# Centred output weights, an addition straight from PSUM, small norm operations on VectorE, and a new table of latencies

## The reference

```python
x = x + layernorm(attn(layernorm(x)))
x = x + layernorm(ffn(layernorm(x)))

def attn(x):
    q = silu(x @ Wq1 @ Wq2)                    # 256 -> 128 -> 512
    f = sigmoid(x @ Wk1 @ Wk2); v = x @ Wv
    a = exp(log_sigmoid(f)); k = 1 - a
    h = scan over tokens of  h = a*h + k*v
    out = q * h
    out = out * rsqrt(mean(out*out) + 1e-6) * norm_w
    return out @ Wo                            # 512 -> 256

def ffn(x):                                    # six blocks
    for i in range(6):
        x = gelu(x @ W1[i].T + B1[i]) @ W2[i].T + B2[i] + x
        if i < 5: x = layernorm(x) * LN_G[i] + LN_B[i]
```

## Time and profile before

| | us |
|---|---|
| median of three runs | 656.39 |
| lowest, highest | 656.38, 657.34 |
| the profiled execution's own time | 656.95 |
| its span, first to last instruction | 655.2 |

### The profile page before, as it was taken

The page is one execution under the profiler, slowest core; times in us unless marked ns, Lnnn a source line. Parts: engine busy times, 40 slices in busy tenths (PEclk is TensorE's granted clock), DMA queues, the critical chain, the costliest instruction groups (busy, mean ns, idle before and its releaser), DMA issues.

```text
span 655.2 us, 8823 instructions
## 1 busy us (share of the span) xinstructions
PE 637.2 (97%) x3015; PEld 530.1 (81%) x3015; DVE 448.2 (68%) x747; ACT 409.7 (63%) x678; POOL 284.2 (43%) x253
## 2 busy tenths in 40 slices
PE   7898999999999999999999999999999999999996
PEld 5677788888888888888888888888888888888886
DVE  6778665678567767758765777677687757764635
ACT  4988986788756555557555575555675545564433
POOL 6988442669516611338232175212372321222203
PEclk9999999999999999999999999999999999999999
DMA  8120000001101200003000021000020000000001
GB/s 283 66 97 1 1 1 1 1 1 66 65 0 48 82 1 2 0 1 117 13 2 0 1 64 66 1 1 1 0 66 1 0 2 0 2 1 32 33 1 66
DMA packets 8685, 19.36 MB, mean 30 GB/s; under 512 B 1600, under 2 KB 4672, under 8 KB 8640
## 3 DMA queue, kind: packets, MB, share of 16 engines
q1 hardware_dynamic: 8352, 18.53, 8.4%
q10 hardware_dynamic: 288, 0.26, 0.1%
HBM read 16.69 MB, written 2.10 MB: 29 GB/s over the span
## 4 chain that ended last, share of the span: by engine, by line
PE 89%; POOL 5%; issue 3%; DVE 1%; ACT 1%; DMA 0%; POOLq 0%; ACTq 0%; DVEq 0%
PE BK L457 43%; PE BK L742 39%; PE BK L566 2%; PE BK L752 2%; POOL WL L344 1%; POOL QB L551 1%; POOL SB L575 1%; PE BK L431 1%; PE BK L612 1%; PE BK L579 0%; POOL WL L298 0%; DMA X<-in_x 0%; PE BK L792 0%; PE BK L629 0%; ACT R L384 0%
## 5 line engine op out<-in xcount | busy, mean ns | idle before, releaser
L728 ACT ACTIVATE HH<-BK,B 128x512 fp32r<-128x512 f32 x192 | 132.4, 690 | 203.7 <-PE BK L457 203.3
L734 DVE TENSOR_TENSOR HL<-BK,HH 128x512 fp32r<-128x512 f32 x192 | 131.0, 684 | 82.6 <-ACT BK L731 82.2
L457 PE MATMUL BK<-XH,WL 128*128 128x512 f32 x416 | 163.7, 393 | 0.0
L457 PE MATMUL BK<-XH,WH 128*128 128x512 f32 x416 | 162.3, 390 | 0.0
L457 PE MATMUL BK<-XL,WH 128*128 128x512 f32 x416 | 162.0, 389 | 0.0
L742 PE MATMUL BK<-HH,WL 128*128 128x512 f32 x368 | 146.7, 399 | 0.0
L742 PE MATMUL BK<-HL,WH 128*128 128x512 f32 x368 | 143.7, 390 | 0.0
L742 PE MATMUL BK<-HH,WH 128*128 128x512 f32 x368 | 143.2, 389 | 0.0
L731 ACT ACTIVATE BK<-BK,B 128x512 f32<-128x512 f32 x192 | 125.6, 654 | 0.0
L457 PEld LDWEIGHTS BK<-XH,WH 128*128 128x128 f32 x416 | 78.1, 188 | 17.0
L457 PEld LDWEIGHTS BK<-XL,WH 128*128 128x128 f32 x416 | 78.2, 188 | 16.1
(11 more groups left out here) (121 smaller groups left out, 823.3 us busy)
## 6 DMA issues: line engine op xcount, KB each, us to landing
STG<-in_w SPq DMA_DIRECT2D x24, 512.0 KB, 3.7
out<-R SPq DMA_DIRECT2D x16, 128.0 KB, 1.9
X<-in_x SPq DMA_DIRECT2D x3, 512.0 KB, 7.8
R<-in_wv SPq DMA_DIRECT2D x1, 512.0 KB, 5.8
STG<-in_wo SPq DMA_DIRECT2D x1, 512.0 KB, 6.2
X<-in_x ACTq DMA_DIRECT2D x2, 128.0 KB, 3.0
X<-in_x SPq DMA_DIRECT2D x2, 128.0 KB, 2.8
R<-in_wq SPq DMA_DIRECT2D x1, 256.0 KB, 3.3
```

Of the source, the lines that this page charges most:

```text
L457: r = e.matmul(dst, s, m, start=first and i == 0, stop=last and i == len(todo) - 1)
L728: lambda e, ev=ev, hs=hs, bias=bias: e.activation(HH[:, hs, :], bank_of[ev][:, :], ACT.Gelu, bias=bias),
L734: lambda e, ev=ev, hs=hs: e.tensor_tensor(HL[:, hs, :], bank_of[ev][:, :], HH[:, hs, :].bitcast(f32), ALU.subtract), ("hlo", n, j))
```

## The change

- **Wo is centred.** Row means of Wo over its 256 output features are subtracted before it is scaled by norm_w and split. The projection then has mean zero over features, so l2 needs no subtraction of a mean. The scaling moves from one GpSimd operation to VectorE: a sum (128x1024 to 128x4), a multiplication by -1/256, and four operations of 128x256 that add the mean and multiply by norm_w. They wait until `ulo` of tile 0 is issued, and have keys from -3.
- **l2_nm is gone.** In its place `x1`, four on VectorE, computes X = PA * RS + X straight from the accumulators. The GpSimd addition is gone, and the next tile's first projection (and the feed-forward pass 2) waits for x1.
- **Small operations.** VE goes to VectorE for all three norms; NM is gone; NBS = mean * -1 * RS is one VectorE operation, and is not made for l2. The power stays on GpSimd. `first_norm` and the norms of the last passes (688, 802) are as they were.
- **Keys.** l3's statistics, norm and transposes get lower keys (Z + 6, 9.5, 11 for Z + 7, 11.5, 13).
- **The planner.** `LASTS` has other durations, `HOP` goes from 0.21 to 0.07, and a table `FREE` is new: the planner gives an engine free that much before the end of its instruction. A DMA issue counts 0.45 for 0.1.

```diff
-LASTS = {"sync": 0.1, "scalar": 0.6, "vector": 0.68, "gpsimd": 1.31, "tensor": 1.36,
-         "_st": 0.41, "_mv": 0.15, "_nm": 0.42, "_rs": 1.03, "_ve": 0.2, "_ng": 0.2, "_nb": 0.2, "ms": 0.15,
-         "turn": 0.88, "zk": 0.69, "zq": 0.69, "rms": 0.45, "proj": 1.44, "t2": 0.72, "scan": 1.31, "olo": 0.85,
...
-         "ghi": 0.69, "gf": 0.65, "ctr": 0.84, "xlo": 0.8, "sum1": 1.41, "sum2": 1.41, "mu": 0.15, "va": 0.15,
-         "vae": 0.15, "rsd": 3.0, "ft": 0.25, "fin0": 0.4, "fin1": 0.83}
-HOP = 0.21
+LASTS = {"sync": 0.45, "scalar": 0.62, "vector": 0.68, "gpsimd": 1.3, "tensor": 1.52,
+         "_st": 0.41, "_mv": 0.16, "_nm": 0.6, "_rs": 1.05, "_ve": 0.16, "_nb": 0.16, "ms": 0.16,
+         "turn": 0.6, "turned": 0.6, "zk": 0.84, "zq": 0.84, "rms": 0.6, "proj": 1.6, "ua": 1.07, "u": 0.62,
+         "t1": 0.6, "t2": 0.72, "a": 0.73, "scan": 1.28, "olo": 0.8, "o": 1.32, "ssum": 1.36,
...
+         "wo_scaled": 0.41, "wo_sum": 1.15, "wo_mean": 0.16, "bias": 0.23, "nw": 0.22,
+         "sum1": 1.45, "sum2": 1.45, "mu": 0.27, "va": 0.27, "vae": 0.16, "rsd": 2.92, "nn": 0.74, "y": 0.74,
...
+FREE = {"sync": 0.0, "scalar": 0.11, "vector": 0.09, "gpsimd": 0.05, "tensor": 0.16}
+HOP = 0.07
 LAND = 2.1
 RATE = 3e5
@@
-        clock[e] = t + (0.1 if done in moved else lasts(e, done))
+        spent = 0.45 if done in moved else lasts(e, done)
+        clock[e] = t + spent - FREE[e]
         if done:
             issued.add(done)
-            ends[done] = clock[e]
+            ends[done] = t + spent
             if done in moved:
-                wire = max(wire, clock[e]) + moved[done] / RATE
+                wire = max(wire, t + spent) + moved[done] / RATE
@@
-        op("scalar", -98, [("one",)], lambda e: e.activation(WARM[:, :], ONE[:, :], ACT.Gelu), ("warm",))
+        op("scalar", -96.5, [("one",)], lambda e: e.activation(WARM[:, :], ONE[:, :], ACT.Gelu), ("warm",))
@@
-        op("gpsimd", -2, [("ldw_o",), ("nw",)],
-           lambda e: e.tensor_tensor(STG[:, 0, :].rearrange("p (m n) -> p m n", m=4),
-                                     STG[:, 0, :].rearrange("p (m n) -> p m n", m=4),
-                                     NW[:, :].unsqueeze(2).to_broadcast([128, 4, 256]), ALU.mult),
-           ("wo_scaled",))
-        split(0.5, raw["o"], WH[:, 1, 2560:3584], WL[:, 1, 2560:3584], "wo", [("wo_scaled",)])
+        op("vector", -3, [("ldw_o",), ("after", ("ulo", 0, 1))],
+           lambda e: e.tensor_reduce(WM[:, :], STG[:, 0, :].rearrange("p (m n) -> p m n", m=4),
+                                     mybir.AxisListType.X, ALU.add), ("wo_sum",))
+        op("vector", -2.9, [("wo_sum",)],
+           lambda e: e.tensor_scalar(WM[:, :], WM[:, :], -1 / 256, 1.0, ALU.mult, ALU.mult), ("wo_mean",))
+        for m in range(4):
+            op("vector", -2.8 + 0.1 * m, [("wo_mean",), ("nw",)],
+               lambda e, m=m: e.tensor_scalar(STG[:, 0, 256 * m:256 * m + 256], STG[:, 0, 256 * m:256 * m + 256],
+                                              WM[:, m:m + 1], NW[:, m:m + 1], ALU.add, ALU.mult), ("wo_scaled", m))
+        split(0.5, raw["o"], WH[:, 1, 2560:3584], WL[:, 1, 2560:3584], "wo", [("wo_scaled", m) for m in range(4)])
@@ stats
             if name == "l2":
-                op("gpsimd", key + gap * 4 + 0.5, [*every, ("ms", t)],
+                op("vector", key + gap * 4 + 0.5, [*every, ("ms", t)],
                    lambda e: e.tensor_tensor(VE[:, t, :], MV[:, t, :, 1], MS[:, t, :], ALU.add), (name + "_ve", t))
             else:
-                op("gpsimd", key + gap * 4 + 0.5, every,
+                op("vector", key + gap * 4 + 0.5, every,
...
-            op("gpsimd", key + gap * 4 + 0.55, every,
-               lambda e: e.tensor_scalar(NM[:, t, :], MV[:, t, :, 0], -1.0, 1.0, ALU.mult, ALU.mult), (name + "_ng", t))
...
-            op("gpsimd", key + gap * 4 + 0.7, [(name + "_rs", t), (name + "_ng", t)],
-               lambda e: e.tensor_tensor(NBS[:, t, :], NM[:, t, :], RS[:, t, :], ALU.mult), (name + "_nb", t))
+            if name != "l2":
+                op("vector", key + gap * 4 + 0.7, [(name + "_rs", t), *every],
+                   lambda e: e.scalar_tensor_tensor(NBS[:, t, :], MV[:, t, :, 0], -1.0, RS[:, t, :], ALU.mult, ALU.mult),
+                   (name + "_nb", t))
@@ proj
-                   + ([("after", ("proj", t, m - 1))] if m else [("l2_nm", t - 1, c) for c in range(4)] if t else []), proj, ("proj", t, m))
+                   + ([("after", ("proj", t, m - 1))] if m else [("x1", t - 1, c) for c in range(4)] if t else []), proj, ("proj", t, m))
@@
-            norm(Z + 4.5, "l2", t, R[:, t], p_of, 0.3, [("turned", k) if t == 0 else ("turn", "l1", t, k) for k in range(2)])
             for c in range(4):
-                op("gpsimd", Z + 5.5 + 0.6 * c, [("l2_nm", t, c)],
-                   lambda e, t=t, c=c: e.tensor_tensor(X[:, t, c, :], X[:, t, c, :], R[:, t, c, :], ALU.add),
-                   ("x1", t, c))
-            stats(Z + 7, "l3", t, x_of, lambda c, t=t: [("x1", t, c)], 0.4)
-            norm(Z + 11.5, "l3", t, R[:, t], x_of, 0.3, [("x1", t, c) for c in range(4)])
-            turn(Z + 13, "l3", t, [("l3_nm", t, c) for c in range(4)], ("mm1", t, 7))
+                op("vector", Z + 4.5 + 0.4 * c, [("l2_rs", t), *x_in(c)],
+                   lambda e, t=t, c=c: e.scalar_tensor_tensor(X[:, t, c, :], p_of(c), RS[:, t, c:c + 1], X[:, t, c, :],
+                                                              ALU.mult, ALU.add), ("x1", t, c))
+            stats(Z + 6, "l3", t, x_of, lambda c, t=t: [("x1", t, c)], 0.4)
+            norm(Z + 9.5, "l3", t, R[:, t], x_of, 0.3, [("turned", k) if t == 0 else ("turn", "l1", t, k) for k in range(2)])
+            turn(Z + 11, "l3", t, [("l3_nm", t, c) for c in range(4)], ("mm1", t, 7))
@@ mm2 of pass 2
-                            [("l2_nm", NT - 1, c) for c in range(4)] if n == 2 else
+                            [("x1", NT - 1, c) for c in range(4)] if n == 2 else
```

More of the change, by code:

```diff
@@ L28 @@
 F_STEP = 2.62
[L32 to L38 removed]
+LASTS = {"sync": 0.45, "scalar": 0.62, "vector": 0.68, "gpsimd": 1.3, "tensor": 1.52,
+         "_st": 0.41, "_mv": 0.16, "_nm": 0.6, "_rs": 1.05, "_ve": 0.16, "_nb": 0.16, "ms": 0.16,
+         "turn": 0.6, "turned": 0.6, "zk": 0.84, "zq": 0.84, "rms": 0.6, "proj": 1.6, "ua": 1.07, "u": 0.62,
+         "t1": 0.6, "t2": 0.72, "a": 0.73, "scan": 1.28, "olo": 0.8, "o": 1.32, "ssum": 1.36,
+         "f_rs": 0.75, "f_nm": 0.41, "x1": 0.47, "ghi": 0.7, "gf": 0.66,
+         "wp_hi": 1.06, "wv_hi": 1.06, "wo_hi": 1.06, "wq1_hi": 0.42, "wk1_hi": 0.42,
+         "wp_lo": 1.45, "wq2_lo": 1.45, "wk2_lo": 1.45, "wv_lo": 2.4, "wo_lo": 2.4, "wq1_lo": 0.42, "wk1_lo": 0.8,
+         "wo_scaled": 0.41, "wo_sum": 1.15, "wo_mean": 0.16, "bias": 0.23, "nw": 0.22,
+         "sum1": 1.45, "sum2": 1.45, "mu": 0.27, "va": 0.27, "vae": 0.16, "rsd": 2.92, "nn": 0.74, "y": 0.74,
+         "ft": 0.38, "inj": 1.9, "end": 1.6, "fin0": 0.41, "fin1": 0.75,
+         "mhalf": 0.1, "quarter": 0.1, "half": 0.1, "one": 0.06, "warm": 2.9, "idle_in": 0.53, "spin": 5.7}
+FREE = {"sync": 0.0, "scalar": 0.11, "vector": 0.09, "gpsimd": 0.05, "tensor": 0.16}
+HOP = 0.07
 LAND = 2.1
@@ L221, in sandwich @@
         MS = sb("MS", [128, NT, 4])
-        NM = sb("NM", [128, NT, 4])
+        WM = sb("WM", [128, 4])
         NBS = sb("NBS", [128, NT, 4])
```

1 line of the change is left out of this document (removed).

## The result

The changed kernel took 661.3 us in the median (661.06 to 662.05, four runs), the kernel before 656.47 beside it: a ratio of 1.0072 with a 95% interval of 1.0055 to 1.009. It is 4.8 us slower, where 4.6 us faster was predicted. The profiled execution has a span of 660.0 us against 655.2.

The account below looks back on a forecast made before the run. PE, busy 97% of the span, was taken as the bound, so gains come from its idle time at 10 to 72 us; -1.8 - 1.0 - 1.7 - 1.2 + 0.7 + 0.4 = -4.6 us gave 651.8 us, range 647.5 to 658.0.

Parts of the forecast that it names:

- first projections: PE's waits for OL and XH at the first projections: shorter with small operations off GpSimd, 0 to 3.0 us, taken 1.8.
- last projection of tile 0: PE's wait for OL after tile 0's fourth scan: GpSimd's relief starts the product earlier, gain 0 to 1.2 us, taken 1.0.
- l2 of tile 0: PE's 2.5 us wait for the accumulators' last read: x1 on VectorE ends it sooner, 0 to 2.5 us, taken 1.7.
- l3 of tile 0: PE's 1.5 us wait at tile 0's third norm: chain 4 us shorter, gain 0 to 1.5 us, taken 1.2.
- Wo block's length: Sum, mean and scalings added on VectorE ahead of attention work at about 15 us: cost 0 to 3.0 us, taken 0.7.
- lock: Small two-operand VectorE operations wait for long GpSimd ones on a shared SBUF port: at most 2.1 us, taken 0.4.
- after 72 us: Rest of the span: VectorE still has room, so reordering costs only if PE waits for a bank; no cost counted.
- o can start about 1.2 us earlier at least: First attention product on GpSimd, at 25.61 us before: without small operations ahead of it, starts about 1.2 us earlier.
- costs nothing: Wo's low part made about 4 us later frees a weight slot later; taken as covered, otherwise 4 us.
- GpSimd as the bottleneck: From 10 to 72 us GpSimd, busy 52.90, was as full as PE; its busy time should fall by 8 us or more.
- B: Rival, chance 0.17: the Wo block on VectorE delays the first tile 3.0 us, gaps behind OL and XH stay; 659 us.
- the first scan after 24 us: Sign that the wo term is wrong, with PE idle near 20 us; the first scan started at 21.97 before.

Follow-up runs that it names:

- e9: Changed kernel in its planned order, Wo block left out, so Wo is neither centred nor scaled: 661.69 us, ratio 1.0059.
- e10: Changed kernel in its planned order, wo_lo and eight feed-forward weight subtractions on GpSimd replaced by zero writes that read nothing: 657.53 us, ratio 0.9997.
- e11: Kernel before in its planned order, the same GpSimd subtractions replaced by zero writes that read nothing: 655.84 us, ratio 0.9978.
- e14: Kernel before in its kept order, only VE and NBS put on VectorE and NM gone: 658.11 us, ratio 1.0007.
- e1: Changed kernel, its order planned with the table of durations of the kernel before: 661.87 us, ratio 1.0068.
- e2: Kernel before, no instruction changed, planned with the new durations, FREE and HOP: 664.09 us, ratio 1.011.
- e3: Kernel before with only the Wo block moved to VectorE, planned anew with the old table: 664.04 us, ratio 1.01.
- e4: Kernel before with only VE and NBS on VectorE and NM gone, planned anew with the old table: 667.98 us, ratio 1.0161.
- e8: Kernel before, planned anew with only the planned start of tile 1's attention changed, 20.6 for 20.4: 658.46 us, ratio 1.0023.
- e18: Kernel before in its kept order, x1 from PSUM on VectorE in all four tiles, Wo not centred, l3's statistics behind the scan: 656.19 us, ratio 0.9986.
- e5: Changed kernel's order, with tile 1's statistics, norm, transposes and first products moved ahead of the Wo block and first projection: 660.67 us, ratio 1.0052.

## Why the prediction was wrong

The sum came out with the wrong sign. Each term, with what came; the measured figures are sums over starts, as above, for the stretch named:

| term | forecast | measured |
|---|---|---|
| first projections | -1.8 | +5.7 (20 to 40 us), an estimated 1 to 1.5 of it the clock |
| last projection of tile 0 | -1.0 | -1.4 (40 to 50 us): the wait of 1.21 us is gone |
| l2 of tile 0 | -1.7 | -1.4 (50 to 60 us): its wait is 0.82 for 2.46 |
| l3 of tile 0 | -1.2 | -0.1 (60 to 72 us): its wait is gone, waits for OL (1.13) and XL (1.04) came |
| Wo block's length | +0.7 | 0 to 0.9, in this order (e9) |
| lock | +0.4 | about +3.5 of the loss, part of the first line (e10, e11) |
| after 72 us | 0 | +2.5 |

**The step that failed first** is "o can start about 1.2 us earlier at least". It was worked out in the order of before: take the small operations away, and everything behind them moves up. Even there it fails: e14 keeps that order, and o starts 0.27 us earlier and not 1.2, because the freed queue then waits for a scan that the small operations on VectorE have made late. And the kernel after doesn't run in that order. The first o starts at 26.31, later than 25.61, and it no longer is what the projection waits for, which is OH behind tile 1's norm and OL behind two more scans. The prediction named the new planning and priced it only beyond 72 us; in the first 72 it followed each chain as if nothing else were placed anew. Experiments e1 to e4 and e8 show that planning anew can have the largest price: +1.5 us for a shift of 0.2 us in one start, +7.2 for new durations with not one instruction changed. In the kept order the parts are worth +0.5 (small operations) and -0.9 (x1 in e18), and in the new one the Wo block at most 0.9. The Wo block in the kept order, and both kept-order edits in one kernel, weren't run.

**The second is the size of the lock.** It was priced for small operations that wait, 2.1 us at most, of which 0.4 went into the sum. What weighs is the other kind: long scans and OL held by long GpSimd subtractions. The scans alone are 8 x (1.709 - 1.244) = 3.7 us longer in the first stage, in the earlier trace rows the first of them 1.32 and now 2.07. For the first scan the cause is that wo_lo slid from 15.41 to 20.63, from before the scans to beside them; e9 puts this down to where the new plan sets Wo's high part on ScalarE, not to the time that the Wo block takes. The prediction, which found that the later wo_lo "costs nothing", looked only at who waits for it, not at whom it would run beside.

**The third is GpSimd as the bottleneck.** Its busy time did fall, 52.90 to 43.39, and it was of no use: its products now wait for the scans.
```profile
POOL QB L562 <- DVE SB L559: 8.0, 4, 4.5
```
That wait was 2.5 us before. VectorE, fuller by 9.7 us, is now the fullest engine of this stage.

**The fourth is the cover after 72 us.** "Costs only if it makes PE wait for a bank": none of the losses there is a wait for a bank. Four are for the sums of the feed-forward norm, which VectorE now brings late once in each of four blocks, 0.25 us more than before; the waits from 150 to 600 us, empty before:
```profile
PE BK L622 <- DVE P L619: 1.0, 4, 0.3
```
The 1.5 us from 72 to 200 us are in steps too small for the list of waits; what causes them wasn't settled. In e10 they are 0.8.

**The rivals.** B, "VectorE takes over: slower", gave 659 for a measured 661.3 and had the direction, and the gap behind OL. Its price was right by accident: it blamed the Wo block's length, which e9 finds to be worth little in the new order, and its sign to look for, the first scan after 24 us, did not show (22.06, against 21.97). In the new order tile 1's statistics and wo_lo come late; that the block's presence made the planner set them so is argued and not tested. What was right: l2's mechanism (from the start of its power to the last read of the accumulators 3.08 us for 4.31 before, 1.2 us less for 1.3 forecast), the relief of GpSimd, and the sign "NBS on VectorE of 1 us and more" (1.24 at 63.94, 1.14 for VE). The last projection came near its forecast by luck: its product was to start up to 4 us earlier and starts at 43.14 for 42.63; in e14 it starts at 42.65, and the wait stays (1.14). In the changed kernel PE is by then some 5 us late itself, and so waits less for it. In e5, where 20 to 40 us cost 4.1 us less, 40 to 72 us cost 2.1 more, which suggests that a part of the 3.1 us won there is only the lateness of PE. "PE's idle time from 10 to 72 us stays at 10 us" was named as what would make the whole wrong; it is 11.4.

**What stays open.** How much of the loss is the planner's luck and how much is in the edits: in the order that the changed kernel has, about 3.5 us are shown to go through GpSimd's reads beside VectorE, and an estimated 1 to 1.5 through the clock, and these overlap; but e1 loses 4.5 us with scans that are hardly longer. New start times for the changed kernel weren't searched; the same edits with fitted ones might do better than e18.

## What to carry to other kernels

An order made by a list scheduler and tuned by its start times is part of the kernel: any edit that plans anew, even one that changes no instruction, can cost more than the edit gains. So price the edit and the plan apart, by making the edit in the frozen order first (here -0.9 and +0.5 us for two of the three parts, against +4.7 for all). When work moves between VectorE and GpSimd, ask of each long GpSimd operation that reads SBUF which two-input VectorE operation will run beside it after the move; and ask in what queue a tiny operation stands, since NBS (0.13 us), behind a scan, left ScalarE idle for 2.56 us.
